# Expert pages in rings of sixteen, expert numbers loaded eight at a time, and page rows issued from the scalar engine's queue

## What is computed

```python
x = layernorm(x + self_attention(x))              # 16 heads of 16
x = layernorm(x + context_attention(x, ctx_1024)) # trilinear similarity, 4 x 256 features -> 256
x = layernorm(x + ffn(x))
# ffn, for each token: 160 experts, the best 8 by sigmoid(x @ router_w.T + bias)
h1 = silu(einsum('th,eih->eti', x, w_gate))       # 256 -> 128, one expert
routed = einsum('eti,ehi->th', h1 * weight_of_expert, w_down)   # 128 -> 256
shared = silu(x @ w_gate_shared.T) @ w_down_shared.T
```

## Time and profile before

| | |
|---|---|
| Three executions | 1271.98, 1276.5, 1289.57 us; median 1276.5 |
| The profiled execution | span 1272.0 us; no time of its own is given beside the span, and the fastest of the three is the same number |
| Instructions | 18559 |
| PE busy | 848.9 us, 67% |
| DVE, ACT, POOL busy | 549.6, 461.4, 359.7 us |
| HBM | read 142.14 MB, written 103.19 MB |

### The profile page before, as it was taken

How to read it: one execution, slowest core, us unless ns; L and a number is a source line. 1 busy time by engine, 2 the same in 40 slices (tenths; PEclk the granted TensorE clock), 3 DMA queues, 4 the chain that set the end, 5 groups by cost and what they waited for, 6 DMA issues and landing times. The chain is left out here.

```text
span 1272.0 us, 18559 instructions
## 1 busy us (share of the span) xinstructions
PE 848.9 (67%) x4116; PEld 565.5 (44%) x4116; DVE 549.6 (43%) x1437; ACT 461.4 (36%) x966; POOL 359.7 (28%) x364
## 2 busy tenths in 40 slices
PE   8558999999769873757630036766676766666492
PEld 4324444444247552544420025555564655555371
DVE  2155666666032783866938112222222222222187
ACT  4305555556531713505212013333333333333211
POOL 4000000000000035163262445455445445454300
PEclk9858999999978996977965569899989889988797
DMA  7999999998511122221021447778787888787693
GB/s 224 261 202 242 247 250 254 255 258 236 168 45 39 50 76 83 75 79 71 30 93 45 125 139 221 226 233 239 233 249 197 253 251 264 239 254 218 208 422 116
DMA packets 154540, 234.37 MB, mean 184 GB/s; under 512 B 26216, under 2 KB 102546, under 8 KB 150178
## 3 DMA queue, kind: packets, MB, share of 16 engines
q1 hardware_dynamic: 135490, 198.04, 55.3%
q0 software_dynamic: 16896, 33.76, 7.3%
q10 hardware_dynamic: 2112, 2.10, 0.5%
HBM read 142.14 MB, written 103.19 MB: 193 GB/s over the span
## 5 line engine op out<-in xcount | busy, mean ns | idle before, releaser
L1369 POOL DMA_INDIRECT contributions<-e_y,e_tail x224 | 218.3, 975 | 235.9 <-ACT e_y L1355 148.2
L1298 PE MATMUL e_psx<-c_ident,e_x 128*128 128x128 f32 x448 | 97.2, 303 | 184.0 <-DMA e_x<-row_pool 180.3
L1503 POOL DMA_INDIRECT row_pool<-rows,places x128 | 127.7, 998 | 270.9 <-issue 151.9
L435 DVE TENSOR_REDUCE a_mx<-a_psS 128x2 f32<-128x1024 f32 x128 | 152.0, 1220 | 112.1 <-PE a_psS L320 110.9
L1308 PE MATMUL e_psg<-e_xt,e_w 128*128 128x128 f32 x896 | 159.5, 305 | 32.0 <-DVE e_xt L1335 14.4
L412 ACT ACTIVATE a_e<-a_psT 128x512 f32<-128x512 f32 x256 | 131.5, 604 | 93.8 <-PE a_psT L342 93.7
L1298 PEld LDWEIGHTS e_psx<-c_ident,e_x 128*128 128x128 f32 x448 | 64.2, 154 | 226.0 <-DMA e_x<-row_pool 137.6
L1335 DVE COPY e_xt<-e_psx 128x256 f32<-128x256 f32 x224 | 93.2, 424 | 149.2 <-PE e_psx L1298 116.3
L1308 PEld LDWEIGHTS e_psg<-e_xt,e_w 128*128 128x128 f32 x896 | 132.5, 212 | 48.8 <-issue 24.0
L1347 ACT ACTIVATE e_g<-e_psg 128x128 f32<-128x128 f32 x224 | 62.1, 277 | 245.0 <-PE e_psg L1308 173.6
L1316 PE MATMUL e_psy<-e_w,e_g 128*128 128x256 f32 x448 | 145.7, 410 | 2.5 <-issue 1.7
(11 more groups left out here) (184 smaller groups left out, 1068.3 us busy)
## 6 DMA issues: line engine op xcount, KB each, us to landing
e_w<-w SPq DMA_DIRECT2D x224, 256.0 KB
row_pool<-fill SPq DMA_DIRECT2D x48, 774.0 KB, 10.9
e_x<-row_pool SPq DMA_DIRECT2D x56, 516.0 KB
c_c<-contributions SPq DMA_DIRECT2D x16, 1024.0 KB, 14.2
a_k<-k_parts SPq DMA_DIRECT2D x32, 256.0 KB
v_heads<-p_v SPq DMA_DIRECT2D x4, 1024.0 KB, 7.1
a_q<-q_parts SPq DMA_DIRECT2D x16, 256.0 KB
a_q<-q_parts SPq DMA_DIRECT2D x32, 128.0 KB
```

Source lines behind the costliest of these rows:

```text
L435: nc.vector.tensor_reduce(mx[:, at.slot, qt, 2 * pair:2 * pair + 2], psS[:, pair], AX, ALU.max).then_inc(maxed, 1)
L1298: last = nc.tensor.transpose(psX[:, at.k % 2, c * P:(c + 1) * P], X[:, at.slot, c * P:(c + 1) * P], ident[:])
L1369: nc.gpsimd.indirect_dma_start(out=contrib, out_offset=bass.IndirectOffsetOnAxis(ap=tail[:, f.slot, 1:2].bitcast(U32), axis=0), in_=Y[:, f ...
L1503: nc.gpsimd.indirect_dma_start(out=pool, out_offset=bass.IndirectOffsetOnAxis(ap=place[:, t, k:k + 1], axis=0), in_=rows[:, t, k], in_offs ...
```

## The change

`ROUND` becomes 16, and with it all the rings and the length of a round. The pool stays at 288 pages. The register loads of a round become two, each of eight expert numbers (`EG = 8`), on SP. The loads of rows leave SP's stream and become part of ACT's, at the head of ACT's step n for every n that four divides; their waits come along, and the first of them takes over the wait for `last_sent`. More semaphores are needed for the longer rings (16 for the weights, 16 for the contributions, 4 for the rows), so `project` hands back the numbers of its own and `mix` clears them with one instruction on POOL.

```diff
-ROUND = 8
+ROUND = 16
...
+        return range(aux_in.num, stored[1].num + 1)          # project
...
+            pool_eng.sem_clear(spent)                        # mix, POOL
...
-    RING, XG = ROUND, 4
+    RING, XG, EG = ROUND, 4, 8
...
         @block.sync
-            def load_rows(at):
-                sp.dma_start(X[:, at.slot:at.slot + XG],
-                             pool[bass.ds(at.n * P, XG * P)].rearrange("(k p) r -> p k r", p=P)
-                             ).then_inc(x_in[at.slot // XG], 16)
+            page_experts = [None] * EG
 
             def step(at):
-                if at.k % XG == 0 and not at.first(RING):
-                    sp.wait_ge(turned, at.n - (RING - XG))
-                    sp.sem_inc(x_loading, 1)
-                    sp.wait_ge(tail_done, at.group(XG) - (RING // XG - 1))
-                    sp.sem_inc(x_loading, 1)
-                    load_rows(at)
                 if not at.first(RING):
                     sp.wait_ge(downed, at.n - (RING - 1))
                     sp.sem_inc(w_loading, 1)
-                e = sp.value_load(table[0:1, bass.ds(at.n, 1)], min_val=0, max_val=EXPERTS - 1)
+                if at.k % EG == 0:
+                    _, page_experts[:] = nc.values_load_multi_w_load_instructions(
+                        table[0:1, bass.ds(at.n, EG)], engines=[mybir.EngineType.SP], min_val=0, max_val=EXPERTS - 1)
+                e = page_experts[at.k % EG]
                 sp.dma_start(W[:, at.slot], w[bass.ds(e, 1)].rearrange("a p n -> (a p) n")).then_inc(w_in[at.slot], 16)
-                if at.fixed and at.n == RING - 1:
-                    sp.wait_ge(last_sent, 16 * TT * TOP_K)
-                    for n in range(0, RING, XG):
-                        load_rows(At(0, n, RING))
...
         @block.scalar
+            def load_rows(at):
+                act.dma_start(X[:, at.slot:at.slot + XG],
+                              pool[bass.ds(at.n * P, XG * P)].rearrange("(k p) r -> p k r", p=P)
+                              ).then_inc(x_in[at.slot // XG], 16)
+
             def step(at):
+                if at.k % XG == 0 and at.within(POOL_PAGES):
+                    if at.first(RING):
+                        if at.n == 0:
+                            act.wait_ge(last_sent, 16 * TT * TOP_K)
+                    else:
+                        act.wait_ge(turned, at.n - (RING - XG))
+                        act.sem_inc(x_loading, 1)
+                        act.wait_ge(tail_done, at.group(XG) - (RING // XG - 1))
+                        act.sem_inc(x_loading, 1)
+                    load_rows(at)
                 f = at.back(1)
                 if f.within(POOL_PAGES):
                     act.wait_ge(gated, at.n)
```

More of the change, by code:

```diff
@@ L542, in load, with mix @@
             sp.dma_start(dst[:], src).then_inc(self.weights_in, 16)
-def mix(nc, inputs, x, ctx_t, ctx_r, od, rows, place, dispatch, last_sent, pool_filled, x2d, pages_d):
+def mix(nc, inputs, x, ctx_t, ctx_r, od, rows, place, dispatch, last_sent, pool_filled, x2d, pages_d, spent):
     with ExitStack() as ctx:
@@ L1493, in decoder_layer @@
             zero = heads.enter_context(nc.sbuf_tensor("a_zero", [HG, HG, S], F32))
-            project(nc, xt, wq, wk, wv, kaux, Q, K, zero, fill, qd, kd, vd)
+            spent = project(nc, xt, wq, wk, wv, kaux, Q, K, zero, fill, qd, kd, vd)
             attend(nc, consts[:, COL["ident"]], Q, K, zero, qd, kd, vd, od, fill, pool, pool_filled, inputs.load)
@@ L1506, in dispatch @@
                     oob_is_err=False).then_inc(sent, 16)
-        mix(nc, inputs, x, ctx_t, ctx_r, od, rows, place, dispatch, last_sent, pool_filled, x2d, pages_d)
+        mix(nc, inputs, x, ctx_t, ctx_r, od, rows, place, dispatch, last_sent, pool_filled, x2d, pages_d, spent)
         tokens = Tokens(nc, ctx, consts[:, COL["ident"]], x2d)
```

## The result

The changed kernel took 1497.8 us (median of 4, 1492.5 to 1501.9) against 1274.8 before (also a median of 4, with a fourth execution of 1273.2 us beside the three known at the forecast): a ratio of 1.1721, 95% interval 1.1652 to 1.1789, slower by 223 us. The forecast of 1440 was right in direction and mechanism and 58 us short in size. The profiled execution is the slowest of the four, 1501.9 us, and its span is 1500.0 us.

The account below looks back on a forecast made before the run. SP's stream was taken to bound the kernel, the contributions' ring close beside. A group's 6.3 + 0.6 + 4.0 = 10.9 us against 7.87, over 55 groups, adds 167 us, less 2.6 at the end: 1440 us, range 1355 to 1500.

Parts of the forecast that it names:

- What bounds the kernel before: Pages: SP's stream sets the pace, 7.87 us a group; the contributions' ring of eight is a second limit close beside.
- Alone this would be worth most of the stalls: SP's stream: fewer register loads and checks, rows' loads gone; SP no longer sets the pace, saving most listed stalls.
- The lead: Rows' load on ACT: cannot issue before PE finishes its previous step; lead zero, PE idles from issue to landing, 55 groups.
- B: From the start of ACT's copy of page n+1 to the rows' issue: 0.6 us a group, ends 0.4 and 1.1.
- C: From the rows' issue to PE's transposes: 4.0 us a group, ends 3.2 and 5.6.
- A: From a group's first transposes to the start of ACT's copy of page n+1: 6.3 us, ends 4.4 and 7.3.
- The rule on the queues: DMA engines alternate between queues, so rows on their own queue need not stand behind weights: C 3.3 us, near 1400 us.
- R1: Rival, pages: clock stays up and rows land quickly, 8.7 us a group, 1320 us; chance 0.13.
- R4: Rival, deeper rings: sixteen weight loads in flight slow the rows, C 5.6, 13.8 us a group, 1600 us; chance 0.03.
- R3: Rival, faster: rows' load does not wait for ACT's copy, DMA engines bound at 301 GB/s, 1179 us; chance 0.03.
- The end: After the last page: passed-over iterations fall from 8 to 4, saving about 2.6 us of PE's 5.30 us stand.
- The contributions: DVE's wait for contributions to land, 159.3 us behind the eight-page ring, is gone behind a sixteen-page ring.

Follow-up runs that it names:

- the first set: Four follow-ups measured beside a kernel before of 1195.2 us: rows_on_sp, act_lead8, only_act, and the kernel before with only the eight-number register loads.
- act_lead8: Changed kernel with the rows' loads still on ACT but issued eight pages (two groups) ahead: 1083.9 us, 0.9079 of before.
- only_act: Kernel before with only the rows' loads moved to ACT's stream, rings of 8 and per-page register loads kept: 1483.8 us, 1.2425 of before.
- rows_on_sp: Changed kernel with the rows' loads back in SP's stream, rings of 16 and eight-number register loads kept: 1088.0 us, 0.9098 of before.

## Why the prediction was right, and where its sum was short

*What bounds the kernel before*: half right. SP's stream was the limit, and I called the ring of contributions "a second limit close beside it". The row I took for proof doesn't show it, though: the instruction with the median of 17 ns has the same median in the changed kernel, where SP waited 391.1 us at that place, so its length says nothing of waiting. What shows it is the view of SP's own waits over the pages of before, which has one line:

```profile
SPq L1268 <- PE e_psx L1298: 7.1, 1, 7.1
```

"Alone this would be worth most of the stalls", of the lighter SP, did not hold: alone it gave 1.0162, the longer rings alone 0.9973, and both together, with the rows on SP, 0.9098. The traces agree that each was hidden behind the other: with the register loads alone DVE waits for contributions, with the rings alone SP has no pause but one. What is missing is the rings alone in the first set, where SP had few stalls; that they would have given nothing there too isn't shown.

*The lead*: right. The load was issued behind ACT's copy in every group, 0.56 us on average, and PE stood 5.2 us (forecast 4.5 to 5). It was shown from both sides: the move alone makes the loss (1.2425), and the lead alone takes it away and the gain appears (0.9079).

*The sum*: forecast 6.3 + 0.6 + 4.0 = 10.9, measured 6.71 + 0.56 + 4.60 = 11.87. B is right. C was mis-sized by 0.6 us, 33 us in 55 groups. I chose it under the median of before "for at the slower pace there is less traffic". On average there is (157 GB/s, not 235), but at the instant that counts there is not: SP, now quick, sends four weight loads as PE frees their slots, and in every other group the rows go out right behind the last. From 1133.30 to 1139.00, while PE waits for the second group shown above, 240 GB/s move. Without the weight loads C is 4.02. (The longest C of before was 5.64, not the 5.44 of the earlier trace rows; the end of 5.6 allowed for it.) A was mis-sized by 0.4, 23 us. I had taken it from the group of the earlier trace rows with its 2.64 us of idle; after 5 us and more the first pages are at the lower clock for longer: in the groups with the longer landing the clock over A is 0.67 and A 6.96, in the others 0.71 and 6.48, where the earlier trace rows had 6.43. Together they are 56 us and B gives 2 back, of the 58 missing.

*The rule on the queues*. The Trainium skill, DMA: Bandwidth & Descriptors (Queues, rings and completion order), says that each DMA engine takes turns between the queues that have work. Read as the forecast reads it, a load on its own queue would have had a C near 3.3. No group from the fourth on came under 3.72 in the changed kernel, and without any weight load the mean is still 4.02. A queue of its own did not save the rows from the weights' traffic; whether it saved a part of the delay isn't shown.

*R1* (clock up, quick landing) missed in both. *R4*, the deeper rings, had a grain of it: weights in flight did lengthen C, to 4.60 on average and not 5.6. *R3* was not the changed kernel's case, but its price of 1179 rested on 301 GB/s, from dividing the rate by the busy share; the kernels with a lead moved 355 to 358 over the pages. *The end* gave 3.0 us where 2.6 was forecast, and the semaphores' clear can't be seen: in the first set the first weight load came at 685.7 us in *act_lead8*, which has it, and at 686.6 in *only_act*, which hasn't. *The contributions*: DVE's wait for them is gone at the pace of the changed kernel; at 4.99 us for a group it is there again behind the ring of 16, in short waits of 2.4 us at most (69.7 us in *rows_on_sp*, from 740 to 1000 us).

## What to carry to other kernels

When an issue moves to another engine's stream, find what that stream must have waited for by then: a deep ring gives no lead to a load that stands, in program order, behind its consumer's previous step. Move the issue point forward (here two groups) together with the queue. And if one of two limits in a row is lifted and nothing happens, try both before giving either up.

## What was not expected

- Lifting the DMA share from 0.78 to 1.01 raised the rate from 235 to 355 GB/s, over the 301 that a division by the share promises, so a busy share is no linear measure of room.
- An eight-number register load and its checks hold SP's stream for 2.8 us (from 1120.88 to 1123.76 in the changed kernel; 2.7 at least, 2.9 in the median), and by that happen to keep weights away from the rows in every other group.
- PE kept busy with work for nothing made the changed kernel 4 to 5% faster (1.1109 of before against 1.1534 and 1.1721) where it would else idle 5 us in each group.
